# S4 convolution and LSTM kernel: convolution operands of groups 1 to 15 as pairs of float16 parts, and weights' low parts taken against SBUF

## The reference, cut to what matters

```python
x = r                                        # (8, 2048, 512) float32
x = x + layernorm(attn(layernorm(x)))        # the convolution
x = x + layernorm(ffn(layernorm(x)))         # the LSTM-like scan

def attn(r, ...):
    K = dplr_kernel(B, C, P, Q, Lam, step)   # one kernel of 2048 taps for each of 512 channels
    h1 = irfft(rfft(r) * rfft(K))[:2048]     # causal convolution along the sequence
    return gelu(h1 + D[0] * r)

def ffn(x, ...):                             # 8 steps over the batch axis, 2048 rows each
    f = sigmoid(x_t @ wf.T + c @ uf.T + bf)
    i = sigmoid(x_t @ wi.T + c @ ui.T + bi)
    g = tanh(x_t @ wc.T + c @ uc.T + bc)
    c = f * c + i * g
    out = tanh(x @ wo.T + c_final @ uo.T + bo)
```

## Time and profile before

| what | value |
| --- | --- |
| median of 3 runs | 2649.8 us (2649.52 to 2650.55) |
| the profiled execution's own time | 2650.23 us |
| its span, first to last instruction | 2648.6 us |
| mean granted TensorE clock | 0.982 |
| PE busy | 2526.6 us (95%) |
| DVE, ACT, POOL busy | 1841.0, 1623.0, 1133.2 us |
| DMA | 542.52 MB, mean 205 GB/s |

### The profile page before, as it was taken

One profiled execution on the slowest core, in us unless ns is written; L12 is line 12 of the kernel. 1 busy time (PEld: TensorE's weight loads), 2 busy tenths in 40 slices (PEclk: granted clock), 3 DMA queues, 4 the chain that ended last, 5 costly groups with the idle time before them and its releaser, 6 DMA issues.

```text
span 2648.6 us, 57574 instructions
## 1 busy us (share of the span) xinstructions
PE 2526.6 (95%) x22659; PEld 2205.2 (83%) x22659; DVE 1841.0 (70%) x3413; ACT 1623.0 (61%) x3003; POOL 1133.2 (43%) x1437
## 2 busy tenths in 40 slices
PE   5499999997899999999999999999999999999997
PEld 4278888886788888888888888888888888888886
DVE  7855556558887677766777887776677764467666
ACT  8656667567665555555556665555555553378777
POOL 7768686725332223222234332322223220068667
PEclk9799999998999999999999999999999999999999
DMA  8779797889674556445655755544555432489998
GB/s 355 286 227 312 267 314 270 271 293 343 181 196 116 130 139 167 119 116 131 141 167 150 204 152 143 166 116 116 135 137 168 119 82 49 168 333 362 370 359 321
DMA packets 507551, 542.52 MB, mean 205 GB/s; under 512 B 273936, under 2 KB 412944, under 8 KB 488720
## 3 DMA queue, kind: packets, MB, share of 16 engines
q1 hardware_dynamic: 507280, 538.85, 65.3%
HBM read 292.88 MB, written 180.88 MB: 179 GB/s over the span
## 4 chain that ended last, share of the span: by engine, by line
PE 84%; DVE 4%; POOL 4%; ACT 3%; DMA 3%; issue 2%; SPq 1%; DVEq 0%; POOLq 0%; ACTq 0%
PE bank L2138 31%; PE bank L2148 29%; PE bank L2194 8%; PE bank L2027 4%; PE bank L1977 3%; PE bank L2013 3%; PE bank L2035 2%; PE bank L1989 2%; PE bank L2169 2%; DVE big L1827 1%; PE bank L1997 1%; ACT big L1343 1%; POOL big L886 1%; POOL big L990 1%; DVE big L1884 1%
## 5 line engine op out<-in xcount | busy, mean ns | idle before, releaser
L2138 PE MATMUL bank<-big 128*128 128x256 f16 x8064 | 1078.8, 273 | 20.8 <-ACT big L1387 8.3
L2148 PE MATMUL bank<-big 128*128 128x256 f16 x7056 | 962.5, 273 | 0.0
L2138 PEld LDWEIGHTS bank<-big 128*128 128x128 f16 x8064 | 790.4, 98 | 117.4 <-ACT big L1387 9.9
L2148 PEld LDWEIGHTS bank<-big 128*128 128x128 f16 x7056 | 690.4, 98 | 79.9
L1031 POOL TENSOR_SCALAR big<-big 128x1 f32<-128x1 f32 x253 | 108.0, 427 | 1084.8 <-DVE big L1674 806.4
L1884 DVE TENSOR_TENSOR big<-bank,big 128x512 f32<-128x512 f32 x256 | 175.1, 684 | 197.1 <-PE bank L2148 195.0
L2194 PE MATMUL bank<-big 128*128 128x256 f16 x2688 | 295.3, 273 | 4.4 <-ACT bank L1323 4.0
L1299 ACT ACTIVATE big<-big 128x512 f32<-128x512 f32 x384 | 289.6, 803 | 13.5 <-DVE big L1884 13.4
L2194 PEld LDWEIGHTS bank<-big 128*128 128x128 f16 x2688 | 262.4, 98 | 37.0 <-ACT bank L1323 4.9
L1870 DVE TENSOR_TENSOR big<-bank,big 128x512 f32<-128x512 f32 x256 | 176.3, 689 | 140.9 <-PE bank L2148 118.5
L1231 ACT ACTIVATE big<-big 128x512 f32<-128x512 f32 x256 | 205.9, 808 | 100.3 <-POOL big L1033 96.5
(11 more groups left out here) (233 smaller groups left out, 3724.3 us busy)
## 6 DMA issues: line engine op xcount, KB each, us to landing
xtd<-big SPq DMA_DIRECT2D x60, 1024.0 KB, 7.0
big<-xr SPq DMA_DIRECT2D x16, 2048.0 KB, 8.7
big<-xg SPq DMA_DIRECT2D x64, 512.0 KB, 7.8
big<-kpad SPq DMA_DIRECT2D x32, 1024.0 KB, 12.2
yd<-big SPq DMA_DIRECT2D x16, 2048.0 KB, 16.8
big<-x SPq DMA_DIRECT2D x128, 256.0 KB, 3.1
x1d<-big SPq DMA_DIRECT2D x128, 256.0 KB, 3.1
big<-x1d SPq DMA_DIRECT2D x64, 512.0 KB, 8.5
```

Of the source, the lines that this page charges most:

```text
L2138: ins = e.matmul(o, WX[2 * g + lw][:, q, kt, 128 * a:128 * a + 128], slot[u % 2][:, part, lx, k0 + kt, :], start=(first and kt == 0 and (l ...
L2148: ins = e.matmul(o, WC[2 * g + lw][:, q, kt, 128 * a:128 * a + 128], cc[unit(u)[1] % 2][:, qc, lx, kt, :], start=False, stop=end, skip_gro ...
```

## The change

It does the following.

- From group 1 on, the input is loaded into one staging buffer `us` of four quarters (the place of the old u[1]), no longer into three buffers in turn. Group 0 keeps its own float32 buffer.
- POOL normalizes as before, in the order of quarters 1, 0, 2, 3, and after the weights' sums. Then, per block of 256 elements, ACT copies the block into float16 (`input_high`) and DVE subtracts this from the block (`input_low`), into the pair buffers u16 (two, by turns, where u[0] and u[2] lay). `SPLIT_AT` gives the steps: blocks 4 and 0 in step 0, 5 and 1, 6 and 2, 7 and 3 in steps 1 to 3, then one block a step in steps 4 to 11 (blocks 8 to 15).
- A quarter of the next group is loaded once its blocks of this group have been split: quarters 1 and 0 at SP's step 4, quarter 2 at step 8, quarter 3 at step 12.
- Each call of `conv_input` becomes three float16 matmuls (groups 1 to 15), and so does `state_in` for blocks 4 and up, with Gm as a pair as well. Blocks 0 to 3 of `state_in` stay float32.
- The taps in kpad become interleaved pairs of float16: DVE scales in place, ACT writes the high parts, POOL the low parts. kpad is written one SP step later.
- The weights' high parts are no longer copied into PSUM (L1211 goes); DVE's low part (L1650) reads the high part in SBUF.
- The four `load_WX` of round 15 move from its start to step 12.

The diff, cut to its core:

```diff
@@ constants
+NORM_ORDER = NORM_FIRST + [4 * g + q for g in range(2, NG) for q in (1, 0, 2, 3)]
+SPLIT_AT = [(4, 0), (5, 1), (6, 2), (7, 3)] + [(k,) for k in range(8, 16)] + [()] * 4
+SPLIT_ORDER = [k for ks in SPLIT_AT for k in ks]
+def split_count(g, k):
+    return 16 * (g - 1) + SPLIT_ORDER.index(k) + 1
@@ buffers
+        u32 = u[0]
+        us = u[1].rearrange("p (q k) h b -> p q k h b", q=4)
+        u16 = [big[:, a:a + 4096].bitcast(F16).rearrange("p (l k h b) -> p l k h b", l=2, k=16, h=G) for a in (u0_at, u2_at)]
+        T16 = [t.rearrange("p h t -> p (h t)").bitcast(F16).rearrange("p (h t l) -> p h t l", h=16, l=2) for t in T]
@@ SP, load_u
-                if g >= 3:
-                    w.wait_ge(s["cv"], G * (g - 2))
+                if g >= 2:
+                    w.wait_ge(s["ulo"], split_count(g - 1, 4 * q + 3))
+                    if q == 0:
+                        w.wait_ge(s["st"], 14 * (g - 1) + 3)
@@ SP, a round
-                for q in range(4):
-                    load_u(4 * (i + 1) + q)
...
                 for j in range(16):
+                    if i < NG - 1:
+                        for q in {4: (1, 0), 8: (2,), 12: (3,)}.get(j, ()):
+                            load_u(4 * (i + 1) + q)
+                    if i == NG - 1 and j == 12:
...
+                        for n in range(4):
+                            load_WX(n)
@@ SP, before the rounds
-                if k == 10:
-                    w.wait_ge(s["kparts"], 1)
+                if k == 11:
+                    w.wait_ge(s["kpair"], 1)
@@ POOL
+                if k == 9:
+                    w.wait_ge(s["kparts"], 2)
+                    c().tensor_tensor(Kp[:, :, 127:255, 1], Ks, Kp[:, :, 127:255, 0], SUB).then_inc(s["pl"], 1)
+                    c("kpair").tensor_copy(Kf[0:32, 0, 127:255], Ks[0:32, 0, :]).then_inc(s["kpair"], 1)
...
+            c("Gh").tensor_copy(Gm16[0], Gm).then_inc(s["Gh"], 1)
+            c("Gh").tensor_tensor(Gm16[1], Gm, Gm16[0], SUB).then_inc(s["Gh"], 1)
             norm(6)
             norm(7)
...
-                for q in range(4):
-                    if i % 4 >= 2 and q == 0:
-                        quarter_sums(i)
+                if i % 4 >= 2:
+                    quarter_sums(i)
+                for q in (1, 0, 2, 3):
                     norm(4 * (i + 1) + q)
@@ ACT
+            def input_high(g, k):
+                w.wait_ge(s["nrm"], norm_place(4 * g + k // 4) + 1)
+                if g >= 2:
+                    w.wait_ge(s["cv"], G * (g - 1))
+                e.activation(u16[g % 2][:, 0, k], us[:, k // 4, k % 4], ACT.Copy).then_inc(s["uhi"], 1)
...
                     if i < NG and j < NP:
                         outm(i, j)
+                    if i < NG:
+                        for k in SPLIT_AT[j]:
+                            input_high(i, k)
                     for step, n, f in WEIGHTS_AT[i, j]:
-                        if step == "lo" and n < 15:
...
-                            e.activation(wbank.rearrange("p (k o) -> p k o", k=2), cut_quarter(f, 0), ACT.Copy).then_inc(s["w_hi"], 1)
@@ DVE
+            def input_low(g, k):
+                w.wait_ge(s["uhi"], split_count(g, k))
+                e.tensor_tensor(u16[g % 2][:, 1, k], us[:, k // 4, k % 4], u16[g % 2][:, 0, k], SUB).then_inc(s["ulo"], 1)
...
+                    if i < NG:
+                        for k in SPLIT_AT[j]:
+                            input_low(i, k)
...
-                                e.scalar_tensor_tensor(cut_quarter(f, 1), wsrc[f], scl[:, 1, g:g + 1], wbank.rearrange("p (k o) -> p k o", k=2), MUL, SUB).then_inc(s["w_lo"], 1)
+                                e.scalar_tensor_tensor(cut_quarter(f, 1), wsrc[f], scl[:, 1, g:g + 1], cut_quarter(f, 0), MUL, SUB).then_inc(s["w_lo"], 1)
@@ PE, state_in
+                if g == 0 or k < 4:
+                    ins = e.matmul(o, Gm, (us[:, 0] if g else u32)[:, k].rearrange("p h b -> p (h b)"), start=True, stop=(k == 0))
...
+                w.wait_ge(s["ulo"], split_count(g, k))
+                for a, (lw, lx) in enumerate(PARTS):
+                    e.matmul(o, Gm16[lw], u16[g % 2][:, lx, k].rearrange("p h b -> p (h b)"), start=(a == 0), stop=False)
@@ PE, conv_input
-                e.matmul(o, T[t % 3][:, h % 16, :], u[g % 3][:, :, h, :], start=(q == 0), stop=False, skip_group_check=True)
+                if g == 0:
+                    e.matmul(o, T[t % 3][:, h % 16, :], u32[:, :, h, :], start=(q == 0), stop=False, skip_group_check=True)
+                    return
+                for a, (lw, lx) in enumerate(PARTS):
+                    e.matmul(o, T16[t % 3][:, h % 16, :, lw], u16[g % 2][:, lx, :, h, :], start=(q == 0 and a == 0), stop=False, skip_group_check=True)
```

More of the change, by code:

```diff
@@ L279, in s4_lstm_program @@
         bank = [ctx.enter_context(nc.psum_tensor(f"bank{i}", [128, 512], F32)) for i in range(8)]
-        kpad = nc.dram_tensor("kpad", (H, 256), F32, kind="Internal")
+        kpad = nc.dram_tensor("kpad", (H, 256), I32, kind="Internal")
         yd = nc.dram_tensor("yd", (NG, 128, B, NK, G), F32, kind="Internal").ap()
@@ L352, in s4_lstm_program @@
         t0_at = top[0]
-        T[0], u[0] = turns16(), rows()
+        T[0] = turns16()
+        u0_at = top[0]
+        u[0] = rows()
         x0_at = top[0]
@@ L360, in s4_lstm_program @@
         conv0 = top[0]
-        T[1], T[2], u[2] = turns16(), turns16(), rows()
+        T[1], T[2] = turns16(), turns16()
+        u2_at = top[0]
+        u[2] = rows()
         x1_at = top[0]
@@ L657, in sync_program @@
                     load_T(i, 0)
[L658 to L662, removed]
-                for j in range(16):
+                for j in range(16):
+                    if i < NG - 1:
+                        for q in {4: (1, 0), 8: (2,), 12: (3,)}.get(j, ()):
+                            load_u(4 * (i + 1) + q)
+                    if i == NG - 1 and j == 12:
+                        w.wait_ge(s["ulo"], 16 * (NG - 1))
+                        w.wait_ge(s["st"], 14 * (NG - 1) + 3)
+                        w.wait_ge(s["wd"], stored(6))
+                        for n in range(4):
+                            load_WX(n)
                     if j == 5 and 2 <= i < NG:
@@ L1173, in act_program @@
                     e.activation(OE[:, 0].rearrange("p f s -> p (f s)"), bank[6][:, 0:256], ACT.Copy).then_inc(s["ak_"], 1)
+                if k == 9:
+                    w.wait_ge(s["kparts"], 1)
+                    e.activation(Kp[:, :, 127:255, 0], Ks, ACT.Copy).then_inc(s["kparts"], 1)
                 if k == 6:
@@ L1976, in state_in @@
                     w.wait_ge(s["ak_"], KERNEL["Gs"])
-                ins = e.matmul(o, Gm, u[g % 3][:, k].rearrange("p h b -> p (h b)"), start=True, stop=(k == 0))
-                if k == 0:
-                    ins.then_inc(s["stin"], 1)
+                if g == 0 or k < 4:
+                    ins = e.matmul(o, Gm, (us[:, 0] if g else u32)[:, k].rearrange("p h b -> p (h b)"), start=True, stop=(k == 0))
+                    if k == 0:
+                        ins.then_inc(s["stin"], 1)
+                    return
+                w.wait_ge(s["Gh"], 2)
+                w.wait_ge(s["ulo"], split_count(g, k))
+                for a, (lw, lx) in enumerate(PARTS):
+                    e.matmul(o, Gm16[lw], u16[g % 2][:, lx, k].rearrange("p h b -> p (h b)"), start=(a == 0), stop=False)
             def state_high(n):
@@ L2021, in conv_input @@
                 w.wait_ge(s[f"T{t % 3}"], 16 * (t // 3 + 1))
-                for piece in range(4 * g, 4 * g + 4):
-                    wait_u(piece)
+                if g:
+                    w.wait_ge(s["ulo"], 16 * g)
+                else:
+                    for piece in range(4):
+                        wait_u(piece)
                 if q == 0 and n >= NC:
                     w.wait_ge(s["gl"], n - NC + 1)
-                e.matmul(o, T[t % 3][:, h % 16, :], u[g % 3][:, :, h, :], start=(q == 0), stop=False, skip_group_check=True)
+                if g == 0:
+                    e.matmul(o, T[t % 3][:, h % 16, :], u32[:, :, h, :], start=(q == 0), stop=False, skip_group_check=True)
+                    return
+                for a, (lw, lx) in enumerate(PARTS):
+                    e.matmul(o, T16[t % 3][:, h % 16, :, lw], u16[g % 2][:, lx, :, h, :], start=(q == 0 and a == 0), stop=False, skip_group_check=True)
             def conv_state(g, h):
```

39 lines of the change are left out of this document (20 added, 19 removed).

## The result

The changed kernel takes 2782.81 us (median of 4 runs, 2778.63 to 2784.28) against 2649.74 us for the kernel before on the same chip: ratio 1.0498, 95% interval 1.0486 to 1.0511, or 133.1 us slower. The forecast was 2763. The profiled execution's span grew from 2648.6 to 2779.7 us.

The account below looks back on a forecast made before the run. PE, busy 95% of the span, was taken to bound the kernel, ACT pacing the early steps. -24 - 2 (ACT) + 136 (DVE behind POOL) + 3 (edges) = +113 on 2650.2 us gave 2763 us, range 2625 to 2830.

Parts of the forecast that it names:

- Part 1: PE in the convolution: float16 input matmuls at 0.053 us, state's input 3 x 0.107; 43 us less at most.
- Rival (b): Strided weights pace PE at 0.107 us per matmul and DVE does not wait: +34, so 2684 us; chance 0.12.
- Part 3: Convolution stage: DVE instructions with both inputs in SBUF wait for POOL's running instruction; plus 136 us.
- Rival (a): Convolution stage: DVE doesn't wait for POOL, the new subtraction takes about 0.43 us; 2627 us, faster; chance 0.20.
- the signs that it named: DVE subtraction's median far from minimum, maxima near 2.7 us, groups near 33 and 41 us, PE idle behind DVE.
- The rows of L1531: Ahead of the convolution: a DVE subtraction took 2.73 us beside POOL, its shape 0.69 elsewhere; taken as the wait's price.
- The 136: Total for DVE waiting behind POOL in the convolution: 39 us plus 97 us in groups with weights.
- POOL's weight sums: In groups with weights, POOL's four sums meet the splits of steps 3 to 5: plus 2.5 us each group.
- steps 7 to 11: Convolution steps said to run at 2.73 us behind POOL: 11.0 us for what takes 7.4, plus 3.6.
- Part 2: ACT in the convolution: 16 copies per group added, seven go with weights; 24 us gained, last round 1.7 more.
- Part 4: Edges of the convolution stage: zero ahead of it, plus 3 us (0 to 8) behind it for moved weight loads.
- Rival (c): PE's gain is exactly eaten by ACT and DVE at every step: 2650 us; chance 0.06.

Follow-up runs that it names:

- the cut normalization: Changed kernel with POOL's normalizing instructions of groups 2 to 15 cut to 8 elements each, everything else kept: 2651.17 us, ratio 1.0002.
- the memsets: Changed kernel with POOL's normalization of groups 2 to 15 replaced by instructions that only write constants: 2652.97 us, ratio 1.0011.
- the last run: Changed kernel with POOL's normalization, ACT's high-part copies of the input and DVE's input subtractions all cut to 8 elements in later groups: 2630.42 us, ratio 0.9928.

## Why the prediction was right and where it was not

**Part 1** was right: 0.055 us per strided conv matmul where 0.053 was taken, 0.107 for the state's input. Rival (b), strided weights at 0.107, is out. The spacing of 81 ns that the Trainium skill gives (TensorE: Matmul & The Clock Gate, Back-to-back issue gap) isn't what these six matmuls show, 0.33 us in all.

**Part 3**, "DVE against POOL, which decides", was right in kind. Rival (a) set its own test, a new subtraction of 0.43 us beside a running normalization; the timeline has 1.85 and 1.80. Of the signs that it named, the maxima came (2.60 and 2.95 us for "near 2.7" and "up to 3"), the groups "near 33 and 41 us" had means of 34.2 and 43.0, and PE waits for DVE's state halves. One did not come: the median of the subtraction is 425 ns, hardly above its minimum of 403, since more than half of the 240 are not held up.

The rows of L1531 were the right ones to price from, and the 0.69 of L1698 was harmless for the reason given. "Every DVE instruction of this stage now has one operand in PSUM" is not quite so, and the exceptions bear the part out. The 32 searches of maxima read one tensor, in SBUF, and never pass 686 ns, before or after, beside POOL too (four from 439.0 us on in the changed kernel, at 0.67). L1641 has two inputs in SBUF, and its nine instructions all ran while POOL was idle, in 0.73 to 0.75 us; in the changed kernel two of the nine (L1686) began inside a normalization and took 2.15:

```profile
L1641 DVE SCALAR_TENSOR_TENSOR big<-big x9: 728/743/752, 172.5 to 406.8; 128x512 f32<-128x512 f32 x9
L1686 DVE SCALAR_TENSOR_TENSOR big<-big x9: 730/748/2151, 181.9 to 487.4; 128x512 f32<-128x512 f32 x9
```

The rule of the Trainium skill (SBUF — State Buffer, Who interferes with whom: an exclusive lock between a DVE instruction with two SBUF inputs and a GpSimd one that reads SBUF) is borne out in both conditions: a PSUM operand frees DVE (at most 430 and 749 ns), and a POOL instruction that only writes (1.80 us each) doesn't hold it.

Its size was low. The 136 hold 17.5 us for POOL's weight sums (7 x 2.5), and these stayed in the runs without normalization. So 118.5 us were forecast for the normalization alone, and the cut normalization gives back 131.6, the memsets 129.8. By rounds: 5.6 us forecast without weights and 6.3 measured, 11.3 with weights and 12.7 measured, 3.6 in round 1 and 2.2 measured. In round 8 the price of a step was right and their number was not: its state low parts in steps 6 to 12 come 16.35 us apart in all, 2.73 a step as forecast, but six steps are held up, 6 to 11, where the sum has four (11.0 us for 7.4; "steps 7 to 11" would be five). A granted clock below full was forecast too: 0.88 in round 10, where PE was busy 32.1 of 43.9 us. Part of that round ran at 1.2 GHz, not 2.4; what this added to the waits in the rounds with weights was not separated. What the sums' waits cost in the changed kernel was not measured by itself.

**Part 2** had a step that failed: "Steps 5 to 15 keep 0.21 each [...] net 2.0 us per group", for the full groups without weights. It costed ACT's 16 copies and did not cost DVE's 16 subtractions of 0.41 us at all, having taken them up only for what they wait. They stand in DVE's list ahead of the next state's low part. With the normalization cut these rounds are 1.3 us shorter than before and not 2.0 (28.87 to 27.47, 29.65 to 28.4), and cutting the subtractions gives 0.8 us a round. Rounds with weights are 0.3 us longer; forecast were 1.3 shorter by part 2 and 2.5 longer by part 3's sums, so 1.2 longer, and they came out better than that. That the last run's 2630 lies close to rival (a)'s 2627 is in part luck: that rival had ACT's copies and the subtractions at full length, and in the run both are short.

**Part 4**: "norms 6 and 7 still end before step 4: zero" failed. The splits begin in step 0 and wait for these norms' instructions, as the chain of the changed kernel shows (start, us, what), and with the other norms cut round 1 is still 3.9 us longer than before, where part 2 had it 1.0 shorter:

```profile
141.31 4.78 DVE big L1645 x2
```

Behind the stage plus 3 was forecast. The chains of the kernel before and of the changed one have the load of y at

```profile
585.01 8.59 DMA big<-yd
714.58 11.70 DMA big<-yd
```

which is 3.1 us more. Round 15 up to this load took 1.1 us more too, where parts 2 and 3 had it even (minus 2.0, plus 2.0), and the rest of the way to the scan some 1.4 less. Ahead of round 1 came 1.2.

**The sum.** +113 forecast, +133.1 measured. The normalization's waits were 13 us above their forecast. The rest, parts 1, 2 and 4 with the sums' waits, was forecast at -5.5 (-23 + 17.5) and stands at +1.5 in the kernel with the normalization cut: 7 more. By its profiled run the rounds without weights were 4.0 above forecast, round 1 4.9, the way from round 15 to the scan 3.1 and the start 0.7, and the rounds with weights 6.0 below. That last error hid part of the others, which is luck. Rival (c), PE's gain eaten at every step, described the size of what is left once POOL is out of the way, but DVE's part in it and not ACT's; it was no outcome for the whole kernel.

## What to carry to other kernels

Before a copy into PSUM is deleted as waste, look at what POOL is doing when its reader runs: the 49 ACT copies of 0.60 us were what let DVE run beside POOL, and leaving them out cost 41 us in the kernel before, and putting them back gave 52 in the changed one. Where a new DVE instruction with two SBUF inputs is to run beside POOL instructions of 2.4 us, give it a PSUM operand, cut POOL's instructions or move the work. And cost a new instruction on every engine that gets one: of the 2.9 us of PE's work that the change saves per round, 16 unhindered subtractions of DVE took 0.8 back, because they stand ahead of the next state's low part.

## What the hardware showed that was not expected

Cutting an engine's work into pieces made it slower by itself and the kernel faster: POOL's 128x1024 takes 2.5 us and four 128x256 take 3.5, waits included, yet the time fell by 87.7 us. Between two POOL instructions back to back DVE gets in with one instruction: at 396.17 and 401.45 the next one waited for a whole further POOL instruction. POOL is held as well, as its L996 of 2.83 us at 398.42 shows, where 2.38 is its length alone. And the gains don't add: the weights' copy gave 52.4 us and the input's PSUM operand 67.8, both together 81.2; with both, most of PE's waiting in the rounds is for ACT.
